# Retention in the token stage: scores, decay and values in another order, with the array quarter innermost

## What is computed

```python
x = x + attention(layernorm(x), ctx, ctx, mask)
# retention, 16 heads of 32
t = layernorm(x);  Q, K, V = heads(t @ Wq), heads(t @ Wk), heads(t @ Wv)
G = swish(t @ Wg + bg)
scores = einsum('bhtd,bhsd->bhts', Q, K) / scale
ret = einsum('bhts,bhsd->bhtd', scores * Dmask, V)      # Dmask: decay, causal
x = x + (layernorm(ret) * gamma + beta) * G @ Wo + bo
# feed forward: bitlinear quantises its input by token, absmax to 127
x = x + bitlinear(gelu(bitlinear(layernorm(x), W1, b1)), W2, b2)
```

## Time and profile before

| | |
|---|---|
| median of 3 runs | 776.42 us (776.38 to 776.57) |
| the profiled execution | 773.9 us, span 772.1 us |
| TensorE busy | 741.4 us, 96% of the span |
| VectorE, ScalarE, GpSimd busy | 53%, 42%, 24% |
| mean granted TensorE clock | 0.993 |
| a turn of the token loop (five of them) | 29.41 us |

### The profile page before, as it was taken

The page is one execution under the profiler, slowest core; times in us unless marked ns, Lnnn a source line. Parts: engine busy times, 40 slices in busy tenths (PEclk is TensorE's granted clock), DMA queues, the critical chain, the costliest instruction groups (busy, mean ns, idle before and its releaser), DMA issues.

```text
span 772.1 us, 18699 instructions
## 1 busy us (share of the span) xinstructions
PE 741.4 (96%) x7464; PEld 608.0 (79%) x7464; DVE 408.4 (53%) x1100; ACT 325.5 (42%) x698; POOL 184.0 (24%) x150
## 2 busy tenths in 40 slices
PE   3999999999999999999999999999999999999985
PEld 2778888888888888988888888778777777777742
DVE  6433333334655534453523333494588788778685
ACT  2436555463353434444344445542343343343232
POOL 1510000003975664754600000011110110110010
PEclk9999999999999999999999999999999999999999
DMA  7141334331322123022121115260000000000001
GB/s 257 70 175 61 112 116 139 111 106 68 115 86 89 58 85 116 31 85 61 31 61 31 33 60 203 73 232 1 1 1 14 14 0 14 14 0 14 0 1 41
DMA packets 33956, 53.63 MB, mean 69 GB/s; under 512 B 2416, under 2 KB 23152, under 8 KB 32656
## 3 DMA queue, kind: packets, MB, share of 16 engines
q1 hardware_dynamic: 29168, 36.05, 14.1%
q0 software_dynamic: 3328, 16.78, 6.1%
q10 hardware_dynamic: 1440, 0.53, 0.3%
HBM read 51.19 MB, written 2.16 MB: 69 GB/s over the span
## 4 chain that ended last, share of the span: by engine, by line
PE 94%; DVE 4%; ACT 1%; issue 1%; DMA 1%; POOL 0%; DVEq 0%; POOLq 0%
PE bank L227 68%; PE bank L550 4%; PE bank L395 4%; PE bank L566 4%; PE bank L409 3%; PE bank L515 3%; PE bank L386 3%; PE bank L503 2%; PE bank L491 1%; PE bank L559 1%; DMA X<-in_x 1%; PE bank L465 1%; PE bank L522 0%; DVE h_max L1221 0%; PE bank L354 0%
## 5 line engine op out<-in xcount | busy, mean ns | idle before, releaser
L227 PE MATMUL bank<-ctx_high,wk_high 128*128 128x258 f32 x512 | 147.6, 288 | 0.0
L227 PE MATMUL bank<-ctx_low,wk_high 128*128 128x258 f32 x512 | 144.8, 283 | 0.0
L227 PE MATMUL bank<-ctx_high,wk_low 128*128 128x258 f32 x512 | 144.3, 282 | 0.0
L227 PEld LDWEIGHTS bank<-ctx_high,wk_high 128*128 128x128 f32 x512 | 96.9, 189 | 13.6 <-issue 13.3
L227 PE MATMUL bank<-wv_high,ctx_high 128*128 128x512 f32 x256 | 106.0, 414 | 0.0
L227 PE MATMUL bank<-wv_low,ctx_high 128*128 128x512 f32 x256 | 101.3, 396 | 0.0
L227 PE MATMUL bank<-wv_high,ctx_low 128*128 128x512 f32 x256 | 100.9, 394 | 0.0
L687 ACT ACTIVATE vals<-bank 128x512 f32<-128x512 f32 x64 | 38.2, 597 | 144.3 <-PE bank L227 144.3
L227 PEld LDWEIGHTS bank<-ctx_low,wk_high 128*128 128x128 f32 x512 | 96.8, 189 | 0.0
L227 PEld LDWEIGHTS bank<-ctx_high,wk_low 128*128 128x128 f32 x512 | 96.6, 189 | 0.0
L677 ACT ACTIVATE kT<-bank,bxk 128x257 f32<-128x257 f32 x128 | 60.1, 470 | 57.4 <-PE bank L227 57.2
(11 more groups left out here) (200 smaller groups left out, 1409.4 us busy)
## 6 DMA issues: line engine op xcount, KB each, us to landing
raw<-in_ctx_t SPq DMA_DIRECT2D x32, 514.0 KB, 4.0
stage<-in_w POOLq DMA_DIRECT2D x16, 1024.0 KB, 5.9
X<-in_x SPq DMA_DIRECT2D x4, 512.0 KB, 7.2
v_last<-last_values SPq DMA_DIRECT2D x32, 64.0 KB
out<-X SPq DMA_DIRECT2D x8, 256.0 KB, 2.0
stage<-in_w_xq SPq DMA_DIRECT2D x1, 1024.0 KB, 8.1
stage<-in_w_xk SPq DMA_DIRECT2D x1, 1024.0 KB, 13.2
stage<-in_w_xv SPq DMA_DIRECT2D x1, 1024.0 KB, 5.6
```

Source lines behind the costliest of these rows:

```text
L227: last = pe.matmul(to, left(i, c), right(j, c), start=(c == 0 and i + j == 0), stop=(c == C - 1 and i == 1))
```

## The change

TensorE, in `tail`: `retention_scores(t)` moves from behind `feed_down(t-2)` to ahead of it. Its loops are turned: group g outside, place j (the quarter) inside, so that four products in a row use four quarters and four banks. It waits at its start for all that it needs, among it the second half of the turned hidden values (`hT_kept`), since banks 5 and 6 hold those before. `retain(t)` gets the same turn of its loops; it waits once for all four decays in place of one by one, and writes bank 4 in place of 7, for which it waits until VectorE has read the output product there (`r_added`). The wait for `ffn_biased`, which guards bank 7, moves to `turn_retained`.

VectorE, in `tail`: the moments of tile t+1, the addition of tile t-1's retention and the moments of tile t-1 come first, then `tn` of tile t+1, then the quantiser of tile t-1 without the gate inside, then the gate, then `decay_scores`, and only then `add_forward(t-2)` and `finish_gate`. GpSimd gives the deviation for the quantised tokens before it adds the bias.

```diff
-            def retention_scores(t):
+            def retention_scores(t, down, more):
...
-                for j in range(HG):
-                    if j == 2:
-                        pe.wait_ge(qkv_kept, 3 * t + 3)
-                    rows = slice(DH * j, DH * (j + 1))
-                    for g in range(C):
+                pe.wait_ge(qkv_kept, 3 * t + 3)
+                if down and more:
+                    pe.wait_ge(hT_kept, 2 * (t - 2) + 2)
+                for g in range(C):
+                    for j in range(HG):
+                        rows = slice(DH * j, DH * (j + 1))
...
-            def retain(t, fed):
+            def retain(t):
+
+                if later(t):
+                    pe.wait_ge(r_added, t)
+                pe.wait_ge(s_decayed, 4 * t + 4)
+                for g in range(C):
+                    for j in range(HG):
+                        h = HG * g + j
+                        last = pe.matmul(bank[4][DH * j:DH * (j + 1), g * P:(g + 1) * P],
...
+                retention_scores(t, down, more)
                 if down and more:
                     feed_down(t - 2)
-                retention_scores(t)
...
                 invert_deviation(t_norm, eps_ln, 1, t + 2, t_moments, t_veps, t_rstd, t + 1)
+                invert_deviation(y_norm, eps_ln, 1, t, y_moments, y_veps, y_rstd, t - 1)
                 add_bias(t + 1)
...
                 if more:
-                    normalise_tokens(t + 1)
+                    measure_tokens(t + 1)
                 if back:
                     add_retained(t - 1, 4)
-                    quantise_tokens(t - 1, lambda: gate(t))
-                else:
-                    gate(t)
+                    measure_normed(t - 1)
+                if more:
+                    scale_tokens(t + 1)
+                if back:
+                    quantise_tokens(t - 1)
+                gate(t)
+                decay_scores(t)
                 if down and more:
                     add_forward(t - 2)
                 finish_gate(t)
-                decay_scores(t)
```

More of the change, by code:

```diff
@@ L492, in turn_queries_keys, with turn_retained @@
                     last.then_inc(qk_turned, 1)
-            def retention_scores(t):
+            def retention_scores(t, down, more):
                 pe.wait_ge(tqT_kept, t + 1)
                 pe.wait_ge(tkT_kept, t + 1)
-                for j in range(HG):
-                    if j == 2:
-                        pe.wait_ge(qkv_kept, 3 * t + 3)
-                    rows = slice(DH * j, DH * (j + 1))
-                    for g in range(C):
+                pe.wait_ge(qkv_kept, 3 * t + 3)
[4 more added lines that the diff above has]
+                        rows = slice(DH * j, DH * (j + 1))
                         last = pe.matmul(bank[S_BANK[j]][:, g * P:(g + 1) * P], tkT[rows, g, :], tqT[rows, g, :],
                                          start=True, stop=True)
-                    last.then_inc(s_ready, 1)
-            def retain(t, fed):
+                        if g == C - 1:
+                            last.then_inc(s_ready, 1)
+            def retain(t):
[6 more added lines that the diff above has]
+                        last = pe.matmul(bank[4][DH * j:DH * (j + 1), g * P:(g + 1) * P],
+                                         v_sb[:, h * DH:(h + 1) * DH], s_sb[:, j, g, :], start=True, stop=True)
+                last.then_inc(retained, 1)
+            def turn_retained(t, fed):
                 if later(fed):
                     pe.wait_ge(ffn_biased, fed)
[L511 to L519, removed]
                 pe.wait_ge(rT_kept, t + 1)
@@ L591, in tail @@
                     turn_quantised(t - 1)
-                retain(t, 0 if not down else t - 1 if more else t - 2)
+                retain(t)
                 if back:
                     feed_up(t - 1, (0, 1))
-                turn_retained(t)
+                turn_retained(t, 0 if not down else t - 1 if more else t - 2)
                 if back:
@@ L813, in tail @@
                 act.wait_ge(retained, t + 1)
-                act.activation(rT_sb[:, :, :], bank[7][:, :].rearrange("p (g n) -> p g n", g=C), ACT.Copy).then_inc(rT_kept, 1)
+                act.activation(rT_sb[:, :, :], bank[4][:, :].rearrange("p (g n) -> p g n", g=C), ACT.Copy).then_inc(rT_kept, 1)
             act.wait_ge(o_projected, T)
@@ L945, in deviations @@
                 invert_deviation(t_norm, eps_ln, 1, t + 2, t_moments, t_veps, t_rstd, t + 1)
+                invert_deviation(y_norm, eps_ln, 1, t, y_moments, y_veps, y_rstd, t - 1)
                 add_bias(t + 1)
-                invert_deviation(y_norm, eps_ln, 1, t, y_moments, y_veps, y_rstd, t - 1)
                 invert_deviation(r_norm, eps_retention, 1, t + 1, r_moments, r_veps, r_rstd, t)
@@ L1108, in moments_of, with measure_tokens, scale_tokens @@
                 dve.bn_aggr(norm[1][:, 0, :], norm[0][:, 0, :]).then_inc(moments, 1)
-            def normalise_tokens(t, between=None):
+            def measure_tokens(t):
                 moments_of(tile(t), t_norm, t_stats, t_moments, t + 1, 4)
-                if between:
-                    between()
+            def scale_tokens(t):
                 dve.wait_ge(t_rstd, t + 1)
@@ L1157, in _ @@
             dve.wait_ge(OT_kept, B)
-            normalise_tokens(0, lambda: output_low(3))
+            measure_tokens(0)
+            output_low(3)
+            scale_tokens(0)
             add_output(3)
@@ L1178, in quantiser, with measure_normed, quantise_tokens @@
                 dve.wait_ge(step, 4 * n + 4)
-            def quantise_tokens(t, between=None):
+            def measure_normed(t):
                 moments_of(tile(t), y_norm, y_stats, y_moments, t + 1, 5)
-                if between:
-                    between()
+            def quantise_tokens(t):
                 dve.wait_ge(y_rstd, t + 1)
@@ L1332, in _ @@
             add_retained(T - 1, 1)
-            quantise_tokens(T - 1, lambda: quantise_hidden(T - 2, 1, last_quant))
+            measure_normed(T - 1)
+            quantise_hidden(T - 2, 1, last_quant)
+            quantise_tokens(T - 1)
             add_forward(T - 3, part=r_sb[:, :])
```

## The result

| | before | after |
|---|---|---|
| median of the runs | 776.40 us (4 runs, 776.09 to 776.57) | 763.07 us (4 runs, 761.97 to 763.88) |
| the profiled execution, its span | 773.9 us, 772.1 us | 763.3 us, 761.2 us |
| mean granted TensorE clock | 0.993 | 0.982 |
| a turn of the token loop | 29.41 us | 26.32 us |

The ratio after to before is 0.9828 (95% interval 0.9811 to 0.9845): faster by 13.3 us, 1.7%. The forecast was 759.2 with a range of 753.9 to 769.5.

What follows compares the result with a forecast made beforehand. TensorE, busy 96% of the span, was taken as the bound. Loop 15.2 us plus single tiles net 2.0 gave 17.2 us, so 776.4 - 17.2 = 759.2 us; range 753.9 to 769.5.

Steps and rivals of the forecast that it cites:

- A pass and its overlap: Scores and values on TensorE: four quarters overlap fully, so scores take 1.10 us instead of 2.75, values 1.01 instead of 2.39.
- two quarters at a time: Rival for scores and values: only two quarters overlap, blocks of 2.06 and 1.98 us, 769.4 us in all; chance 0.08.
- no gain: Rival for both blocks: alternating quarters gains nothing and neither does the order, within 776.4 +- 1.5 us; chance 0.05.
- strict program order: Slower rival: passes start strictly as written, blocks of 3.7 and 2.3 us, 783.4 us in all; chance 0.05.
- The turn: Token loop: each of five turns takes 26.4 us instead of 29.4, gaining 15.2 us.
- The cover of 1.4 us: Loop: all four decays end 1.4 us before TensorE reaches `retain`, so the wait for them costs nothing.
- The second rival: Loop: GpSimd or the quantiser 2 us late, `retain` waits 0.6 us, clock can fall; 770.7 us; chance 0.06.
- The three tiles outside the loop: First, second and last tile gain 1.0, 1.5 and 2.5 us, sum 5.0; net 2.0 after the clock's cost.
- The clock: TensorE idles ahead of `retain` at three single tiles; half clock there costs 1.0 us each, between 0 and 1.7.
- The drain moves as a whole: Drain behind the last tile: same program, only shifted in time, no gain or loss.
- The carried difference: Profiled execution lies 2.5 us below the median of the runs; carried over, making 756.7 into 759.2 us.

Runs made afterwards that it cites:

- both edits: Kernel after, plus unread products filling TensorE's waits at the three single tiles and GpSimd's bias addition held until the quantised tokens are written: 755.35 us, ratio 0.973.
- the first experiment: Kernel before with only the loops of scores and values turned (quarter innermost), its old order kept: 788.48 us, ratio 1.0161.
- the values alone: Kernel after with the scores' loops turned back, so only the values have the quarter innermost: 768.74 us, ratio 0.9913.
- the one kept busy at the tiles alone: Kernel after with unread products in TensorE's waits at the three tiles outside the loop: 757.50 us, ratio 0.9756.
- the bias later: Kernel after with GpSimd waiting until the quantised tokens are written before it adds the bias: 759.91 us, ratio 0.9793.
- the order alone: Kernel after with both blocks, scores and values, turned back to one quarter at a time: 780.11 us, ratio 1.004.

## Why the prediction was right, and where it was off

The sign and the mechanism were right, and the time lies within the range, 3.9 us above the forecast. By its steps:

**A pass and its overlap: right.** 1.10 and 1.01 us were worked out from eight passes of one quarter; the chain shows 1.10 and 1.01. The mechanism is in the trace too: the passes start in eight groups of four (by the order of the loop one for each quarter), the second group 0.21 us behind the first and the others 0.11 us apart. TensorE's timeline of the kernel after, cut at 579.96 and at 580.07:

```profile
579.76 0.39 PE L504 MATMUL bank<-tqT,tkT 32*128 32x128 f32 x4
...
579.76 0.50 PE L504 MATMUL bank<-tqT,tkT 32*128 32x128 f32 x8
```

The rivals of two quarters at a time (2.06 and 1.98), of no gain (2.75 and 2.39) and of strict program order (3.7 and 2.3) fall with that. Nor do passes start strictly as written: in the kernel before, the pass that ends the first quarter of the scores, the eighth as written, is the eleventh to start. The Trainium skill, TensorE: Matmul & The Clock Gate, Part 3, whose factors gave an estimate of 0.90 and 1.01, is met by the values and missed by 0.2 us by the scores (2.75/1.10 = 2.5 times, not 3.07); its factor for columns was measured with three quarters, and the values use four.

**The turn: right.** 26.4 us forecast, 26.32 measured; the loop 15.2 forecast, 15.4 measured. VectorE waits for the turned retained tile 0.76 us (about 1 was forecast).

**The cover of 1.4 us: wrong, without cost in the loop.** It is 0.27. The order of the steps came out as worked out, but the quantiser's first step (`y_sb`) was priced at its 0.54 of the earlier trace rows, where it had no neighbour that hurt it; that is 0.95 of the 1.1 us by which the decays end later. The deviation was moved ahead of the bias, so the step that waits for the deviation now starts together with the bias. The move was costed and the new neighbour was not. The second rival (a new wait in each turn) came within 0.27 us of being true. The same 0.95 us are paid in full at the second tile.

**The three tiles outside the loop: wrong, a term of the sum mis-sized.** The gain without the clock was put at 1.0 + 1.5 + 2.5 = 5.0. Where half clock and contention are taken out (both edits, above) the second and the last stretch are 1.34 and 2.51 shorter than before, and the first tile, 6.89 us from its scores to its successor's first projection, takes 5.94: 0.95. That is 4.8 us, so this part holds. The clock was put at 3 x 1.0, "between 0 and 1.7" each, 1.7 being what the one stretch of the earlier trace rows can cost. It cost 1.43 + 2.03 + 2.86 = 6.3, since the clock stayed down for 6.7 and 6.8 us at two of the three tiles, and not for 3.40 as in the earlier trace rows. The upper bound was read from a single stretch. That the waits were longer here (2.54 and 2.68 us, where it was 0.89 in the earlier trace rows) does not explain it: in the first experiment 3.4 us followed waits of 2.90, and with the values alone the clock stayed down for 6.8 us at the second tile, at waits of 0.88 and 1.01:

```profile
553.40:560.23 6.83, 5.49 (x46) 3.44 (x47) 3.29 (x6) 3.33 (x5) 0.00 (x0) 0.50 0.01 2
```

What sets the length is open.
I also had the second tile's wait in the wrong place: 2.54 us of it is for the gate, whose bank the transposes need, and no term of the sum named that. It costs nothing by itself, since the values wait for the decays behind the gate in any case.

**"The drain moves as a whole": wrong by 1.4 us.** Its program is the same, and it took 38.02 us instead of 36.64. Before, it had two stretches of 3.4 us at half clock, at 747.8 and 761.5; after, one of 3.4 and one of 6.85:

```profile
747.80:751.20 3.40, 3.40 (x12) 1.20 (x10) 3.19 (x9) 1.02 (x1) 0.00 (x0) 0.50 0.00 0
761.50:764.90 3.40, 3.00 (x20) 1.90 (x19) 2.54 (x4) 2.05 (x2) 0.00 (x0) 0.50 0.00 0
```

The time goes with the clock: the same drain took 36.54 us in the run with both edits, again with two stretches of 3.4, and 37.99 in the one kept busy at the tiles alone, with one of 3.4 and one of 6.8. Why the clock stayed down longer the second time is not settled by these runs.

In us of the profiled executions, plus for a gain:

| stretch | forecast | measured |
|---|---|---|
| first tile, with the projections behind it | 1.0 - 1.0 | 0.80 - 1.41 |
| second tile | 1.5 - 1.0 | -1.64 |
| loop | 15.2 | 15.4 |
| last tile | 2.5 - 1.0 | -0.34 |
| drain | 0 | -1.4 |
| ahead of the first tile's scores | 0 | -0.5 |
| sum | 17.2 | 10.9 |

**The carried difference: two measures of the miss.** I added 2.5 us since the profiled execution of before lay that far below the median. It lies below every one of the 23 runs of that kernel beside the experiments (lowest 774.93). The kernel after has its profiled execution 0.2 above its median. So the sum promised 6.6 us too much by the profiled executions (17.2 against 10.6) and 3.9 by the medians (17.2 against 13.3). The 2.7 between them is a difference of executions, and the last column of the table has it too: 0.5 of it stands ahead of the first tile's scores, where the two programs are the same, and where the rest lies is not known.

## What to carry to other kernels

Small products on a part of the array are cheap only if neighbours in the program use different parts; the gain was much the same for the scores, which write four banks, as for the values, which write one (2.5 and 2.4 times). A pass's step and its length could be read from a row of equal passes, and four quarters then cost what one costs. A block made shorter takes cover away from whatever it hid: here the gain turned to a loss of 12 us until the next operand was ordered ahead, and a wait that is left costs its length and can cost a stretch at half clock that is longer than the wait. When a step is moved, price it again beside its new neighbour on another engine, as VectorE beside GpSimd here, and where TensorE must wait at a few single places, products whose result nobody reads can keep its clock up there.

## What the runs showed of the chip

**VectorE beside GpSimd.** A float32 `TENSOR_SCALAR` of 128x512 on VectorE takes 0.54 to 0.55 us, and 1.50 when a GpSimd `TENSOR_TENSOR` on two inputs in SBUF (1.28 us) started 0.06 us ahead of it; it ends 0.28 us after that. The same GpSimd addition beside VectorE's decays (one input a PSUM bank, 2.48 us) changes neither. The Trainium skill, SBUF — State Buffer, "Who interferes with whom", has the rule: a pair of ports is shared by the two engines, `tensor_scalar` can take it, whoever issues first holds it for the whole instruction, and an operation with at most one input in SBUF, outside the two-port modes, does not need it. The trace agrees in kind; by the rule, with nothing done before the end of GpSimd's instruction, the step would have taken an estimated 1.22 + 0.55 = 1.77 us, and it took 1.50.

**TensorE's clock behind short waits.** At waits of 2.5 to 2.9 us the clock fell to half in every case that was not filled, within the wait or close behind it, in five loop turns of five in the first experiment. At shorter waits it sometimes did: at the first tile, behind waits of 1.97 and 0.72, it fell in the kernel after and not with the bias later; at the last tile, at 1.78, with the order alone and not with the values alone. It lasted 3.4 or 6.8 us, and which of the two differed between executions of nearly the same program. Filling the waits with products kept 1.00 and gave 5.6 us at three tiles; filling the drain's gave 1.7 more.
